# Attention vectors of the first graph layer in the tile loop, and the output projection written out by tiles with a ring for x

## The chip, the core and the metric

One core of a Trainium2 chip. The time is the device time of one execution in microseconds (us). The kernel before was run three times: 2285.08, 2288.67 and 2289.95 us, median 2288.67. One more execution was profiled.

## What is computed

A block of a graph transformer on x, 1250 nodes x 768, all in fp32. Only the mixing part and the products with the attention vectors matter here; xn is the layer norm of x.

```
# linear attention with random features (8 heads of 96, 256 features)
q, k, v = split(xn @ qkv_w.T + qkv_b);  q, k = q * scale, k * scale
phi_q, phi_k = exp(q @ rf.T - |q|^2/2), exp(k @ rf.T - |k|^2/2)
kv = phi_k^T v;  attn = (phi_q kv) / max(phi_q . sum(phi_k), 1e-6)
x1 = x + attn @ proj_w.T + proj_b (+ b2 of the graph layers)
# graph attention, first layer (4 heads of 512), second layer (1 head of 768)
al = xn @ wa,   wa[:, side, head]  = sum_c W1[:, head, c] * a_side[head, c]
al2 = h1 @ wa2, wa2[:, side]       = sum_c W2[:, c] * a2_side[c]
```

The edges' softmax and sums, the second layer, a router and 32 experts follow.

## The kernel before, in words

The 1250 nodes are 10 tiles (NT) of 125 rows (P); the 768 columns are 6 slices (KD) of 128. The program is a sequence of stages, each a block in which every engine has its own list of instructions, with waits on semaphores between them; a stage begins when all engines have ended the one before. The order in a stage is written out by hand.

The stages that matter: norm_phase; then, for each half of the heads, the tile loop of mix_half_phase (its `with ExitStack() as st1` block) and the stage `numerator`; then proj_phase; then first_layer_phase, and the rest of the network.

**Tile loop** (lines 641 to 815). For each tile TensorE (PE) multiplies xnT with the half's q, k and v weights (mix_G, L743), turns q and k (mix_TQ, L754), makes k's features (mix_PH, L762) and accumulates kv (mix_KV, L771). Between these it does two "windows" of another job, the counts of edges (mix_count_S, L791), from one-hot tiles that VectorE (DVE) writes into a ring (L667, L673). DVE's order per tile: evacuate q and k (L684), wait for ScalarE (ACT) to square them (L717), reduce to norms (L689), first window, evacuate v (L696), second window. ACT's order: squares, q's copy, counts, k's copy, exponential of the first two heads (L728), counts, exponential of the other two (L731). SyncE (SP) loads the attention vectors a (mix_a) and three 128-row slices of W1 (mix_w_slice) at the start of the stage and stores counts.

**Numerator** (L345 to L430). DVE begins with the half's 24 attention vectors: for each of 3 slices, 2 sides and 4 heads a multiply and sum over 512 columns (L413) into wa; only then does it release the two result banks R (L418, `num_used`). PE takes two heads at a time: 12 matmuls for the features of q into six banks F (L374, each two records), which ACT exponentiates (L398), then the products with kv into R (L384); DVE divides them into attn (L425 to L427). SP issues the next weights: those of half 1, and after half 1 those of the projection (L2101).

**Projection** (L433 to L566). SP loads the two biases, the whole of x (proj_x, L100 and L101), a2 and four chunks of W2 (L462), then stores the rows of x1 (L468). Per tile POOL copies attn's tile into proj_at (L476), PE turns it in six transposes into two banks (L488), ACT and DVE copy them into proj_aT (L518, L528), and PE multiplies with the weights into two banks Y (L497, 24 records). DVE adds the bias to x's row (L532), then Y (L537), and from the third tile on does four products of W2's attention columns (L555) per tile. There is one set of turn banks and one set of Y banks. PE's loop:

```
    turn(0)
    with pe.Fori(0, NT // 2 - 1) as i:
        for b in range(2):
            turn(i * 2 + (b + 1))
            project(i * 2 + b, b)
```

Of the kernel before, what the change touches and what calls it, by code (L numbers as in the profile page):

```python
# [10 lines left out]
ALU = mybir.AluOpType  # L11
# [40 lines left out]
MAX_AT = 5  # L52
NTAB = MAXT + AHEAD + 1
# [291 lines left out]
def numerator(nc, cx, tag, half, rfT, qT, kv, attn, a_loaded, slice_loaded, ws, ab, wa, load_next):  # L345
# [3 lines left out]
    KH = KD // 2  # L349
# [3 lines left out]
    wa_step = cx.sem(tag + "wa_step")  # L353
    with ExitStack() as st:
        junk = sb(nc, st, tag + "junk", [128, 2, C1])
# [46 lines left out]
        def _(dve):  # L402
            step = Chain(dve, dve_step)
            dve.wait_ge(a_loaded, 32)
            n = 0
            for k in range(KH):
                dve.wait_ge(slice_loaded[k], 16)
                for s in range(2):
                    for h in range(H1):
                        if n >= 2:  # L410
                            dve.wait_ge(wa_step, n - 1)
                        col = s * H1 + h
                        dve.tensor_tensor_reduce(out=junk[:, n % 2, :], in0=ws[k][:, h * C1:(h + 1) * C1],  # L413
                                                 in1=ab[:, s, h * C1:(h + 1) * C1], scale=1.0, scalar=0.0,
                                                 op0=ALU.mult, op1=ALU.add,
                                                 accum_out=wa[:, half * KH + k, col:col + 1]).then_inc(wa_step, 1)
                        n += 1
# [15 lines left out]
def proj_phase(nc, cx, attn, w, w_loaded, proj_b, gnn_b2, x, x1_dram, ident, W2, a_src2, a_dst2, wa2):  # L433

    (loaded, x_loaded, staged, turned, copied_a, copied_d, projected, stored, stores) = (
        cx.sem("proj_" + s) for s in ("loaded", "x_loaded", "staged", "turned", "copied_a", "copied_d", "projected",
                                      "stored", "stores"))
    biased = cx.sem("proj_biased")
    a2_loaded, wa2_step = cx.sem("proj_a2_loaded"), cx.sem("proj_wa2_step")
    KC = 4  # L440
    w2_loaded = [cx.sem(f"proj_w2_loaded{c}") for c in range(KF // KC)]
    with ExitStack() as st:
# [4 lines left out]
        xr = sb(nc, st, "proj_x", [P, NT, D])  # L447
        at = sb(nc, st, "proj_at", [P, D])
# [24 lines left out]
        def _(pool):  # L473
            with pool.Fori(0, NT) as t:
                pool.wait_ge(turned, t + 1)
                pool.tensor_copy(at[:], attn[:, bass.ds(t, 1), :]).then_inc(staged, 1)  # L476
# [1692 lines left out]
```

## Time and profile before

| | us |
|---|---|
| median of three runs | 2288.67 |
| lowest, highest | 2285.08, 2289.95 |
| the profiled execution | 2279.98 |
| its span in the trace | 2278.2 |
| busy: PE, DVE, ACT, POOL | 2102.0, 1115.7, 409.6, 184.5 |
| mean granted clock of PE, share of full | 0.951 |

Times in the trace are counted from the start of the span. A row of a timeline gives start, duration, engine, source line, operation, what it writes <- what it reads, and in brackets how long the engine had been idle before and what ended that. A row of busy times gives the stretch, its length, the busy time of PE, PE's weight loads, DVE, ACT and POOL with the number of instructions, the granted clock of PE, the busy share of the DMA engines and GB/s. An fp32 matmul leaves two records. A matmul's end is modelled, so neighbouring groups of PE can overlap by some tenths of a microsecond.

### The profile page before, as it was taken

Reading aid. Unit: us, or ns where it says so; the run is one execution under the profiler, and the core shown is the slowest. Engines: PE = TensorE matmul, PEld = TensorE weight load, DVE = VectorE, ACT = ScalarE, POOL = GpSimd, SP = SyncE. Lnnn points to the kernel's source line nnn. Section 1 sums busy time; section 2 is a strip of 40 time slices with the busy share of each in tenths; the row PEclk is TensorE's granted clock in tenths of the full one; section 3 lists DMA queues with packets and bytes.
Section 4 is the critical chain, followed back from the end, with each engine's and each line's share of the span. In section 5 each row is a group of like instructions: output and inputs, shape, how many; then the busy total and the mean of one; then the engine's idle time right before and its main releaser. Section 6 shows DMA issues by size and latency. Waiting matters only on the chain. (4 is left out here: it accounts for less than half of the span.)

```text
span 2278.2 us, 32891 instructions
## 1 busy us (share of the span) xinstructions
PE 2102.0 (92%) x9786; PEld 1455.2 (64%) x9787; DVE 1115.7 (49%) x2411; ACT 409.6 (18%) x745; POOL 184.5 (8%) x178
## 2 busy tenths in 40 slices
PE   5999899998799998899999799989966999999997
PEld 3666566666444443788888655545563777777776
DVE  6566545654454500888888300236445333333343
ACT  2211212122002311222222100000010122222221
POOL 0000000000000000000000000000001232333222
PEclk9999899999899999899999899999955899999999
DMA  7000220002634511333433354432053688898754
GB/s 240 18 15 18 82 98 18 18 17 82 200 112 134 167 53 45 121 120 94 127 98 95 124 191 148 141 101 55 11 201 119 197 245 249 247 288 253 206 130 76
DMA packets 80399, 282.26 MB, mean 124 GB/s; under 512 B 11268, under 2 KB 31292, under 8 KB 70717
## 3 DMA queue, kind: packets, MB, share of 16 engines
q1 hardware_dynamic: 59309, 216.48, 28.5%
q0 software_dynamic: 14048, 51.06, 9.7%
q10 hardware_dynamic: 6960, 13.62, 1.7%
q8 instruction: 51, 0.84, 0.2%
q14 instruction: 31, 0.25, 0.0%
HBM read 222.26 MB, written 58.87 MB: 123 GB/s over the span
## 5 line engine op out<-in xcount | busy, mean ns | idle before, releaser
L1199 PE MATMUL gat_Z<-h,gat_wt 125*125 125x256 f32 (+1 forms) x1600 | 354.8, 381 | 17.9 <-DVE gat_wt L1115 17.9
L1199 PEld LDWEIGHTS gat_Z<-h,gat_wt 125*125 125x125 f32 x1600 | 298.1, 188 | 63.5 <-DVE gat_wt L1115 18.7
L743 PE MATMUL mix_G<-mix_w,xnT 128*125 128x384 f32 x720 | 242.5, 487 | 0.0
L2017 PE MATMUL ex_PH<-ex_xT,ex_w 128*128 128x128 f32 x1872 | 223.8, 279 | 2.6 <-issue 1.1
L1347 PE MATMUL gat2p_Y<-gat2p_w,gat2p_hT 128*125 128x386 f32 (+1 forms) x640 | 209.7, 489 | 10.3 <-DMA gat2p_w<-in_L_gnn_W 10.3
L2017 PEld LDWEIGHTS ex_PH<-ex_xT,ex_w 128*128 128x128 f32 x1872 | 214.7, 193 | 4.0 <-issue 4.0
L2027 PE MATMUL ex_PY<-ex_w,ex_hT 128*128 128x384 f32 x624 | 214.8, 494 | 1.8 <-ACT ex_hT L1966 1.7
L983 PE MATMUL first_G<-gnn_w,xnT 128*125 128x512 f32 x480 | 208.4, 593 | 0.0
L743 PEld LDWEIGHTS mix_G<-mix_w,xnT 128*125 128x125 f32 x720 | 132.9, 189 | 84.5 <-issue 1.5
L1347 PEld LDWEIGHTS gat2p_Y<-gat2p_w,gat2p_hT 128*125 128x125 f32 x640 | 120.2, 188 | 98.4 <-issue 12.5
L2027 PEld LDWEIGHTS ex_PY<-ex_w,ex_hT 128*128 128x128 f32 x624 | 114.3, 190 | 77.9 <-ACT ex_hT L1966 3.4
L983 PEld LDWEIGHTS first_G<-gnn_w,xnT 128*125 128x125 f32 x480 | 89.0, 188 | 110.4 <-issue 110.4
L1461 PE MATMUL gat_Z<-h,gat_wt 125*125 125x385 f32 (+1 forms) x400 | 132.1, 493 | 9.4 <-DVE gat_wt L1419 9.4
L1461 PEld LDWEIGHTS gat_Z<-h,gat_wt 125*125 125x125 f32 x400 | 75.9, 190 | 65.6 <-DVE gat_wt L1419 10.0
L667 DVE SCALAR_TENSOR_TENSOR mix_count_A<-count_ikey,count_off,keyT 128x512 f32 x120 | 90.2, 752 | 54.0 <-issue 49.6
L673 DVE TENSOR_SCALAR mix_count_B<-count_islo,sloT 128x314 f16 x480 | 112.1, 299 | 0.0
L1937 DVE TENSOR_SCALAR ex_idS<-ex_ids 128x1 int32 x52 | 8.0, 154 | 211.4 <-DMA out_rows<-ex_y,ex_idS 211.4
L1907 DVE SCALAR_TENSOR_TENSOR ex_Q<-posm,offs,ex_iota 125x1280 bf16<-125x1280 f32 x55 | 85.4, 1552 | 42.7 <-issue 38.4
L1888 POOL DMA_INDIRECT out_rows<-ex_y,ex_idS x52 | 82.6, 1588 | 264.8 <-DVE ex_y L1939 217.1
L497 PE MATMUL proj_Y<-mix_w,proj_aT 128*125 128x384 f32 x240 | 81.9, 500 | 12.2 <-DVE proj_x L537 12.2
L791 PE MATMUL mix_count_S<-mix_count_B,mix_count_A 128*128 x480 | 86.5, 301 | 4.2 <-DVE mix_count_B L673 2.1
L1103 DVE TENSOR_TENSOR gat_u<-al,gat_rows 125x1250 f32<-125x1250 f32 x40 | 58.2, 1455 | 55.3 <-DMA gat_rows<-mT_dram 55.3
(292 smaller groups left out, 2212.9 us busy)
## 6 DMA issues: line engine op xcount, KB each, us to landing
ex_w<-in_L_ffn_W SPq DMA_DIRECT2D x64, 1152.0 KB
gat_cnt<-c_dram SPq DMA_DIRECT2D x50, 546.9 KB
gat2p_hT<-h1T_dram SPq DMA_DIRECT2D x20, 1000.0 KB, 5.0
h1T_dram<-gat_oT ACTq DMA_DIRECT2D x40, 250.0 KB, 2.0
mix_w<-in_L_mix_qkv_w SPq DMA_DIRECT2D x6, 1152.0 KB, 13.2
ct_dram<-mix_count_out SPq DMA_DIRECT2D x40, 157.0 KB, 2.2
mix_w_slice<-in_L_gnn_W SPq DMA_DIRECT2D x6, 1024.0 KB, 12.0
proj_w2s<-in_L_gnn_W SPq DMA_DIRECT2D x4, 1536.0 KB, 25.1
```

Of the source, the lines that this page charges most:

```text
L667: dve.scalar_tensor_tensor(CA[:, bass.ds(s * RB, RB), :], ikey[:].unsqueeze(1).to_broadcast([128, RB, 128]), off[:, win:win + 1], keyT[:, ...
L673: last = dve.tensor_scalar(CB[:, bass.ds(s * RB + b, 1), :], islo[:].unsqueeze(1), sloT[:, bass.ds(r * RB + b, 1)], None, ALU.is_equal)
L743: last = pe.matmul(G[c][:], xnT[:, k, t * P:(t + 1) * P], w[:, k, c, :], start=(k == 0), stop=(k == KD - 1))
L791: last = pe.matmul(S[:], CA[:, bass.ds(s * RB + b, 1), :].rearrange("p o k -> p (o k)"), CB[:, bass.ds(s * RB + b, 1), :].rearrange("p o k ...
L983: last = pe.matmul(G[g % 2][:], xnT[:, k, t * P:(t + 1) * P], w[hd % 2][:, k, :], start=(k == 0), stop=(k == KD - 1))
L1199: last = pe.matmul(Z[b][j][:], wt[b][:, s, :], h[:, s, bass.ds(hd, 1), j * HC:(j + 1) * HC + j], start=(s == 0), stop=(s == NT - 1))
L1347: last = pe.matmul(Y[b][j][:, 0:HW if j else W], hT[q % 2][:, k, :], w[:, k, cols], start=(k == 0), stop=(k == KF - 1))
L1461: last = pe.matmul(Z[b][j][:], wt[b][:, s, :], h2[:, s, 385 * j:385 * j + CW[j]], start=(s == 0), stop=(s == NT - 1))
L1888: pool.indirect_dma_start(out, bass.IndirectOffsetOnAxis(ap=idS[:, 0:1], axis=0), y[:], None, compute_op=ALU.add).then_inc(added, 16)
L1907: dve.scalar_tensor_tensor(Q[:], posm[:, :, bass.ds(e, 1)].to_broadcast([P, NT, SLOT]), offs[:, bass.ds(at, 1)], iot[:].unsqueeze(1).to_br ...
L2017: last = pe.matmul(PH[m][:], w1[:, b, k, m * 128:(m + 1) * 128], xT[:, k, :], start=(k == 0), stop=(k == KD - 1))
L2027: last = pe.matmul(PY[j][:], hT[:, k, :], w2[:, b, k, j * 384:(j + 1) * 384], start=(k == 0), stop=(k == KM - 1))
```

## The change

1. **Attention vectors.** The loop leaves `numerator` and comes into DVE's list of the tile loop, behind each tile's second window: tile t does columns t*24//10 to (t+1)*24//10 - 1, two or three. The slices of W1, a and the scratch tile now live in the tile loop's memory.
2. **Ring for x.** proj_x holds 4 tiles instead of 10 and is allocated outside the stage. `load_proj`, issued by SP in the numerator of half 1, loads the first four tiles of x behind the projection's weights. In proj_phase SP stores a tile, waits for the store and loads the tile four further on.
3. **Projection by tiles.** All loops over tiles are written out. POOL's copy is gone: PE turns attn itself. There are two sets of turn banks and two of Y banks; PE begins with turns 0 and 1, ahead of the wait for the weights, then alternates project(t) and turn(t + 2). The W2 chunks are issued one per tile instead of all four at the start.

The core of the diff:

```diff
             step = Chain(dve, dve_step)
-            dve.wait_ge(a_loaded, 32)
-            n = 0
-            for k in range(KH):
-                dve.wait_ge(slice_loaded[k], 16)
-                for s in range(2):
-                    for h in range(H1):
-                        if n >= 2:
-                            dve.wait_ge(wa_step, n - 1)
-                        col = s * H1 + h
-                        dve.tensor_tensor_reduce(out=junk[:, n % 2, :], in0=ws[k][:, h * C1:(h + 1) * C1],
-                                                 in1=ab[:, s, h * C1:(h + 1) * C1], scale=1.0, scalar=0.0,
-                                                 op0=ALU.mult, op1=ALU.add,
-                                                 accum_out=wa[:, half * KH + k, col:col + 1]).then_inc(wa_step, 1)
-                        n += 1
             dve.sem_inc(num_used, 2)
...
-        xr = sb(nc, st, "proj_x", [P, NT, D])
-        at = sb(nc, st, "proj_at", [P, D])
         aT = [sb(nc, st, f"proj_aT{b}", [128, KD, P]) for b in range(2)]
-        TP = [pb(nc, st, f"proj_T{j}", [128, 3, P]) for j in range(2)]
-        Y = [pb(nc, st, f"proj_Y{j}", [P, 384]) for j in range(2)]
+        TP = [[pb(nc, st, f"proj_T{b}{j}", [128, 3, P]) for j in range(2)] for b in range(2)]
+        Y = [[pb(nc, st, f"proj_Y{b}{j}", [P, 384]) for j in range(2)] for b in range(2)]
         block = st.enter_context(nc.Block())
 
         @block.sync
         def _(sp):
             sp.dma_start(bias[:, 0, :], proj_b.partition_broadcast(128)).then_inc(loaded, 16)
             sp.dma_start(bias[:, 1, :], gnn_b2.partition_broadcast(128)).then_inc(loaded, 16)
-            rows_dma(sp, xr, x.rearrange("(t p) d -> p t d", p=P), x_loaded)
             sp.dma_start(a2[:, 0, :], a_src2[0, :].partition_broadcast(128)).then_inc(a2_loaded, 16)
             sp.dma_start(a2[:, 1, :], a_dst2[0, :].partition_broadcast(128)).then_inc(a2_loaded, 16)
-            for c in range(KF // KC):
-                sp.dma_start(w2s[:, c * KC:(c + 1) * KC, :],
-                             W2[c * KC * 128:(c + 1) * KC * 128, :].rearrange("(k p) n -> p k n", p=128)
-                             ).then_inc(w2_loaded[c], 16)
-            with sp.Fori(0, NT) as t:
-                sp.wait_ge(stored, t * 2 + 4)
-                for lo, n in ((0, PM), (PM, P - PM)):
-                    sp.dma_start(x1_dram[bass.ds(t * P + lo, n), :],
-                                 xr[lo:lo + n, bass.ds(t, 1), :].rearrange("p o d -> p (o d)")).then_inc(stores, 16)
-            sp.wait_ge(stores, 32 * NT)
-
-        @block.gpsimd
-        def _(pool):
-            with pool.Fori(0, NT) as t:
-                pool.wait_ge(turned, t + 1)
-                pool.tensor_copy(at[:], attn[:, bass.ds(t, 1), :]).then_inc(staged, 1)
+            for t in range(NT):
+                b = t % XR
+                if t < KF // KC:
+                    sp.dma_start(w2s[:, t * KC:(t + 1) * KC, :],
+                                 W2[t * KC * 128:(t + 1) * KC * 128, :].rearrange("(k p) n -> p k n", p=128)
+                                 ).then_inc(w2_loaded[t], 16)
+                sp.wait_ge(summed, 2 * t + 2)
+                rows_dma(sp, x1_dram[t * P:(t + 1) * P, :], xr[:, b, :], stores[b])
+                if t + XR < NT:
+                    sp.wait_ge(stores[b], 32 * (t // XR + 1))
+                    rows_dma(sp, xr[:, b, :], x[(t + XR) * P:(t + XR + 1) * P, :], x_loaded[b])
+            for b in range(XR):
+                sp.wait_ge(stores[b], 32 * len(range(b, NT, XR)))
 
         @block.tensor
         def _(pe):
-            pe.sem_inc(turned, 1)
-            pe.sem_inc(projected, 4)
-
             def turn(t):
-                pe.wait_ge(staged, t + 1)
+                b = t % 2
+                if t >= 2:
+                    pe.wait_ge(copied_a, t - 1)
+                    pe.wait_ge(copied_d, t - 1)
+                for k in range(KD):
+                    last = pe.transpose(TP[b][k // 3][:, k % 3, :], attn[:, t, k * 128:(k + 1) * 128], ident[0:P, 0:P])
+                last.then_inc(turned, 1)
+
+            def project(t):
+                b = t % 2
                 pe.wait_ge(copied_a, t + 1)
                 pe.wait_ge(copied_d, t + 1)
-                for k in range(KD):
-                    last = pe.transpose(TP[k // 3][:, k % 3, :], at[:, k * 128:(k + 1) * 128], ident[0:P, 0:P])
-                last.then_inc(turned, 1)
-
-            def project(t, b):
-                pe.wait_ge(copied_a, t + 2)
-                pe.wait_ge(copied_d, t + 2)
                 for j in range(2):
-                    pe.wait_ge(stored, 2 * t + (j + 1))
+                    if t >= 2:
+                        pe.wait_ge(summed, 2 * (t - 2) + (j + 1))
                     for k in range(KD):
-                        last = pe.matmul(Y[j][:], aT[b][:, k, :], w[:, k, j * 384:(j + 1) * 384],
+                        last = pe.matmul(Y[b][j][:], aT[b][:, k, :], w[:, k, j * 384:(j + 1) * 384],
                                          start=(k == 0), stop=(k == KD - 1))
                     last.then_inc(projected, 1)
 
+            turn(0)
+            turn(1)
             pe.wait_ge(w_loaded, 16)
-            turn(0)
-            with pe.Fori(0, NT // 2 - 1) as i:
-                for b in range(2):
-                    turn(i * 2 + (b + 1))
-                    project(i * 2 + b, b)
-            turn(NT - 1)
-            project(NT - 2, 0)
-            project(NT - 1, 1)
+            for t in range(NT):
+                project(t)
+                if t + 2 < NT:
+                    turn(t + 2)
 
         @block.scalar
         def _(act):
-            act.sem_inc(copied_a, 1)
-            with act.Fori(0, NT // 2) as i:
-                for b in range(2):
-                    act.wait_ge(turned, i * 2 + (b + 2))
-                    act.wait_ge(projected, i * 4 + (2 * b + 2))
-                    act.activation(aT[b][:, 0:3, :], TP[0][:], ACT.Copy).then_inc(copied_a, 1)
+            for t in range(NT):
+                act.wait_ge(turned, t + 1)
+                if t >= 2:
+                    act.wait_ge(projected, 2 * (t - 1))
+                act.activation(aT[t % 2][:, 0:3, :], TP[t % 2][0][:], ACT.Copy).then_inc(copied_a, 1)
...
             def add(t):
-                row = xr[:, bass.ds(t, 1), :]
-                dve.tensor_tensor(row, row, bias[0:P, 0:1, :], ALU.add).then_inc(biased, 1)
+                row = xr[:, t % XR, :]
+                dve.wait_ge(x_loaded[t % XR], 32 * (t // XR + 1))
+                dve.tensor_tensor(row, row, bias[0:P, 0, :], ALU.add).then_inc(biased, 1)
                 dve.wait_ge(biased, t + 2)
                 for j in range(2):
-                    dve.wait_ge(projected, 2 * t + (j + 5))
-                    col = xr[:, bass.ds(t, 1), j * 384:(j + 1) * 384]
-                    dve.tensor_tensor(col, Y[j][:].unsqueeze(1), col, ALU.add).then_inc(stored, 1)
-
-            turn(0, 0)
-            turn(1, 1)
-            dve.wait_ge(loaded, 32)
-            dve.tensor_tensor(bias[:, 0, :], bias[:, 0, :], bias[:, 1, :], ALU.add).then_inc(biased, 1)
-            dve.wait_ge(x_loaded, 32)
-            dve.wait_ge(biased, 1)
+                    dve.wait_ge(projected, 2 * t + (j + 1))
+                    col = xr[:, t % XR, j * 384:(j + 1) * 384]
+                    dve.tensor_tensor(col, Y[t % 2][j][:], col, ALU.add).then_inc(summed, 1)
...
+            turn(0)
+            turn(1)
+            dve.wait_ge(loaded, 32)
+            dve.tensor_tensor(bias[:, 0, :], bias[:, 0, :], bias[:, 1, :], ALU.add).then_inc(biased, 1)
+            dve.wait_ge(biased, 1)
             for t in range(NT):
                 add(t)
                 if t + 2 < NT:
-                    turn(t + 2, t % 2)
+                    turn(t + 2)
                 if t >= 2:
                     for k in range(2 * (t - 2), 2 * (t - 1)):
                         attention_columns(k)
-
 
...
+                    def attention_column(n):
+                        k, col = n // (2 * H1), n % (2 * H1)
+                        side, hd = col // H1, col % H1
+                        if n == 0:
+                            dve.wait_ge(a_loaded, 32)
+                        if col == 0:
+                            dve.wait_ge(slice_loaded[k], 16)
+                        if n >= 2:
+                            dve.wait_ge(wa_step, n - 1)
+                        dve.tensor_tensor_reduce(out=junk[:, n % 2, :], in0=ws[k][:, hd * C1:(hd + 1) * C1],
+                                                 in1=ab[:, side, hd * C1:(hd + 1) * C1], scale=1.0, scalar=0.0,
+                                                 op0=ALU.mult, op1=ALU.add,
+                                                 accum_out=wa[:, half * KH + k, col:col + 1]).then_inc(wa_step, 1)
+
+                    columns = 2 * H1 * KH
                     pair = ((q_done, q_turned, q_evac, qsq, q_ready), (k_done, k_turned, k_evac, ksq, k_ready))
                     for t in range(NT):
...
                                           brow[0:P, 2, :].rearrange("p (h d) -> p h d", d=MD), ALU.add
                                           ).then_inc(v_evac, 1)
                         window(PER * t + 1)
+                        for n in range(t * columns // NT, (t + 1) * columns // NT):
+                            attention_column(n)
                 dve.wait_ge(kv_step, NT)
...
                 rfT = sb(nc, st2, "mix_rfT", [MD + 1, RF])
+                xr = sb(nc, st2, "proj_x", [P, XR, D])
+                xr_loaded = [cx.sem(f"proj_x_loaded{b}") for b in range(XR)]
                 counting = (sb(nc, st2, "count_ikey", [128, 128]), sb(nc, st2, "count_islo", [128, SLO], F16),
                             sb(nc, st2, "count_off", [128, NW]), sb(nc, st2, "count_zero", [128, 128], BF16))
                 w_proj = w_qkv[:, :, 0:2, :].rearrange("p k c n -> p k (c n)")
                 def load_proj(eng):
                     eng.dma_start(w_proj, ins["L0_mix_proj_w"].rearrange("(k p) n -> p k n", p=128)
                                   ).then_inc(proj_loaded, 16)
+                    for t in range(XR):
+                        rows_dma(eng, xr[:, t, :], x[t * P:(t + 1) * P, :], xr_loaded[t])
 
```

## Rows read from the trace of the kernel before

**Rows 1.** The page's busy times: busy us, share, number of instructions.

```profile
PE 2102.0 (92%) x9786; PEld 1455.2 (64%) x9787; DVE 1115.7 (49%) x2411; ACT 409.6 (18%) x745; POOL 184.5 (8%) x178
```

**Rows 2.** Busy times by stretch, 540 to 600 us; engines, granted clock, DMA share, GB/s.

```profile
540.00:600.00 60.00, 43.93 (x193) 29.64 (x193) 13.58 (x28) 8.15 (x16) 4.12 (x5) 0.86 0.67 201
```

**Rows 3.** PE's timeline, half 0's numerator and entry of half 1: start us, us, what.

```profile
256.56 10.36 PE L374 MATMUL mix_F<-mix_qT,mix_rfT 97*128 x24 [1.91 <-ACTq L391]
269.95 10.61 PE L384 MATMUL mix_R<-mix_kv,mix_phiq 128*125 x80 [3.03 <-DVEq L418]
280.40 8.59 PE L374 MATMUL mix_F<-mix_qT,mix_rfT 97*128 x24
288.83 8.87 PE L384 MATMUL mix_R<-mix_kv,mix_phiq 128*125 x80
300.33 1.57 PE L777 MATMUL mix_KV<-mix_vs,mix_zero 125*128 125x388 f32 x4 [2.63 <-POOL mix_vs L646]
```

**Rows 4.** Busy times by stretch, three stretches of 2 us after a pause.

```profile
272.00:274.00 2.00, 2.00 (x12) 2.00 (x11) 0.81 (x3) 0.00 (x0) 0.00 (x0) 0.50 0.00 0
...
302.00:304.00 2.00, 2.00 (x7) 1.12 (x6) 0.00 (x0) 0.00 (x0) 0.00 (x0) 1.00 1.03 422
...
562.00:564.00 2.00, 1.79 (x7) 1.64 (x8) 0.24 (x1) 0.16 (x1) 0.26 (x2) 0.50 0.83 180
```

**Rows 5.** Timeline, half 1's numerator.

```profile
529.72 10.60 PE L384 MATMUL mix_R<-mix_kv,mix_phiq 128*125 x80 [3.01 <-DVEq L418]
```

**Rows 6.** Groups of instructions of 255 to 272 us: busy us, mean ns.

```profile
L413 DVE CUSTOM_DVE_ANT_0 mix_junk<-mix_w_slice,mix_a 128x512 f32<-128x512 f32 x24 | 14.8, 685 | 0.5 <-PEq L604 0.5
...
L413 DVE DVE_READ_ACCUMULATOR2_ANT gnn_wa<- 128x1 f32 x24 | 1.9, 80 | 0.0
```

**Rows 7.** Timeline, PE from the output projection to the next stage's first matmul.

```profile
560.33 0.83 PE L488 MATMUL proj_T<-ident,proj_at 125*128 125x125 f32 x6 [2.86 <-POOL proj_at L476]
...
585.10 10.01 PE L497 MATMUL proj_Y<-mix_w,proj_aT 128*125 128x384 f32 x24 [12.16 <-DVE proj_x L537]
...
595.59 7.91 PE L497 MATMUL proj_Y<-mix_w,proj_aT 128*125 128x384 f32 x24
...
645.90 15.65 PE L497 MATMUL proj_Y<-mix_w,proj_aT 128*125 128x384 f32 x48
...
667.22 14.66 PE L989 MATMUL mask_T<-xnT,gnn_wa 128*8 128x416 f32 x36 [5.67 <-PEq L94]
```

**Rows 8.** Timeline, DVE's first work on x in the output projection.

```profile
583.50 0.96 DVE L532 TENSOR_TENSOR proj_x<-proj_x,proj_bias 125x768 f32<-125x768 f32 x1 [17.11 <-DMA proj_x<-in_x]
```

**Rows 9.** Busy times by stretch, the output projection once it runs evenly.

```profile
604.00:645.00 41.00, 41.00 (x146) 24.74 (x145) 31.54 (x60) 2.41 (x5) 4.14 (x5) 1.00 0.15 47
```

**Rows 10.** Timeline of one tile of half 0's tile loop.

```profile
144.97 0.55 DVE L684 SCALAR_TENSOR_TENSOR mix_qs<-mix_G,mix_brow 125x384 f32<-125x384 f32 x1
...
146.37 0.56 DVE L684 SCALAR_TENSOR_TENSOR mix_qs<-mix_G,mix_brow 125x384 f32<-125x384 f32 x1 [0.86 <-PE mix_G L743]
...
150.67 0.60 ACT L731 ACTIVATE mix_phik<-mix_PH 125x512 f32<-125x512 f32 x1 [0.50 <-PE mix_PH L762]
...
151.71 0.55 DVE L689 TENSOR_REDUCE mix_nrm<-mix_sq 125x4 f32<-125x384 f32 x1 [4.78 <-ACT mix_sq L717]
...
156.10 0.59 PE L754 MATMUL mix_TQ<-ident,mix_qs 125*97 125x125 f32 x4
```

**Rows 11.** Line L689's idle time and releaser: us, times.

```profile
  ACT mix_sq L717: 86.0, 18
```

**Rows 12.** DVE's timeline, end of half 1's tile loop.

```profile
514.48 1.03 DVE L702 COPY mix_kv<-mix_KV 128x388 f32<-128x388 f32 x2 [7.21 <-PE mix_KV L771]
```

**Rows 13.** DMA issues: number, KB each, median us from issue to landing.

```profile
mix_w_slice<-in_L_gnn_W SPq DMA_DIRECT2D x6, 1024.0 KB, 12.0
proj_w2s<-in_L_gnn_W SPq DMA_DIRECT2D x4, 1536.0 KB, 25.1
...
mix_w<-in_L_mix_proj_w SPq DMA_DIRECT2D x1, 2304.0 KB, 8.2
```

More of the change, by code:

```diff
@@ L52 @@
 MAX_AT = 5
+XR = 4
 NTAB = MAXT + AHEAD + 1
@@ L342, in _, with numerator @@
                 last.then_inc(transposed, 1)
-def numerator(nc, cx, tag, half, rfT, qT, kv, attn, a_loaded, slice_loaded, ws, ab, wa, load_next):
-    KH = KD // 2
+def numerator(nc, cx, tag, half, rfT, qT, kv, attn, load_next):
     HH, A, HT = MH // 2, MD + 1, NT // 2
@@ L430, in _, with proj_phase @@
             step.end(HH // 2)
[L433 to L438, printed above, removed]
+def proj_phase(nc, cx, attn, w, w_loaded, proj_b, gnn_b2, x, xr, x_loaded, x1_dram, ident, W2, a_src2, a_dst2, wa2):
+    (loaded, turned, copied_a, copied_d, projected, summed, biased) = (
+        cx.sem("proj_" + s) for s in ("loaded", "turned", "copied_a", "copied_d", "projected", "summed", "biased"))
     a2_loaded, wa2_step = cx.sem("proj_a2_loaded"), cx.sem("proj_wa2_step")
+    stores = [cx.sem(f"proj_stores{b}") for b in range(XR)]
     KC = 4
@@ L520, in _, with turn @@
         @block.vector
         def _(dve):
-            dve.sem_inc(copied_d, 1)
-            dve.sem_inc(stored, 2)
-            def turn(t, b):
-                dve.wait_ge(turned, t + 2)
-                dve.wait_ge(projected, 2 * t + 2)
-                dve.tensor_copy(aT[b][:, 3:6, :], TP[1][:]).then_inc(copied_d, 1)
+            def turn(t):
+                dve.wait_ge(turned, t + 1)
+                if t >= 2:
+                    dve.wait_ge(projected, 2 * (t - 1))
+                dve.tensor_copy(aT[t % 2][:, 3:6, :], TP[t % 2][1][:]).then_inc(copied_d, 1)
@@ L550, in attention_columns @@
                     dve.wait_ge(a2_loaded, 32)
-                for s in range(2):
-                    n = 2 * k + s
+                for side in range(2):
+                    n = 2 * k + side
                     if n >= 2:
                         dve.wait_ge(wa2_step, n - 1)
-                    dve.tensor_tensor_reduce(out=junk[:, s, :], in0=w2s[:, k, :], in1=a2[:, s, :], scale=1.0,
+                    dve.tensor_tensor_reduce(out=junk[:, side, :], in0=w2s[:, k, :], in1=a2[:, side, :], scale=1.0,
                                              scalar=0.0, op0=ALU.mult, op1=ALU.add,
-                                             accum_out=wa2[:, k, s:s + 1]).then_inc(wa2_step, 1)
+                                             accum_out=wa2[:, k, side:side + 1]).then_inc(wa2_step, 1)
+            turn(0)
[3 more added lines that the diff above has]
+            dve.wait_ge(biased, 1)
             for t in range(NT):
@@ L601, in mix_half_phase @@
         kv = sb(nc, st, tag + "kv", [128, HH, 2, A])
-        ws = [sb(nc, st, tag + f"w1_slice{k}", [128, F1]) for k in range(KD // 2)]
-        ab = sb(nc, st, tag + "a", [128, 2, F1])
         with ExitStack() as st1:
+            ws = [sb(nc, st1, tag + f"w1_slice{k}", [128, F1]) for k in range(KH)]
+            ab = sb(nc, st1, tag + "a", [128, 2, F1])
+            junk = sb(nc, st1, tag + "junk", [128, 2, C1])
             qs = sb(nc, st1, tag + "qs", [P, 2, HH, A])
@@ L816, in _ @@
                         keys_values(t, not more)
-        numerator(nc, cx, tag, half, rfT, qT, kv, attn, a_loaded, slice_loaded, ws, ab, wa, load_next)
+        numerator(nc, cx, tag, half, rfT, qT, kv, attn, load_next)
 def first_layer_phase(nc, cx, W1, xnT, wa, ident, al, alT_dram, ct_dram, c_dram, mask_dram, mT_dram, h):
```

9 lines of the change are left out of this document (4 added, 5 removed).

## The prediction

> **What bounds the kernel now.** I read the page's busy times first: TensorE (PE) is busy for 92% of the span [rows 1], so time can be won only where PE stands still or runs at a low clock. The busy times by stretch come next. They show the worst stretch of the part that the diff touches: between 540 and 600 us PE is busy for 43.93 us of 60, at a mean granted clock of 0.86, while the DMA engines are 67% busy [rows 2]. Last I read the order of work there.
>
> In the numerator of half 0, PE ends its feature matmuls (mix_F) at 256.56 + 10.36 = 266.92. Its next group (mix_R) starts at 269.95, after 3.03 us of waiting for VectorE's (DVE's) sequencer at L418, which is the line behind the 24 attention vectors [rows 3]. The same group takes 10.61 us the first time and 8.87 the second [rows 3]; in between lies a stretch at a granted clock of 0.50, which is 1.2 of 2.4 GHz [rows 4]. Half 1 repeats this: 3.01 us of wait, then 10.60 us [rows 5]. The vectors are 24 instructions of DVE with a mean of 685 ns, and as many short reads of the accumulator of 80 ns, which overlap their neighbours: 14.8 us for the 24 [rows 6].
>
> In the output projection, PE starts its first transposes at 560.33 after waiting for POOL's copy. It stands still for 12.16 us before 585.10, until DVE has added the first tile, and the 24 matmuls that follow take 10.01 us where undisturbed ones take 7.91 [rows 7]. DVE itself had waited 17.11 us for the load of x [rows 8]. From 604 us on there is no wait: PE is busy for 41.00 of 41.00 us, DVE for 31.54 [rows 9].
>
> **Part 1, the attention vectors leave the numerator.** DVE then reaches L418 at once. The ACT engine's last exponentials feed the second head, not the first group, so nothing else holds mix_R, as in the second pass, where it starts 0.16 us before the modelled end of mix_F [rows 3]. Gone are the gaps, 3.03 + 3.01 us. With no gap there is no cause for the low clock behind it: I price mix_R at the 8.87 us of its second pass, which saves 1.74 + 1.73 us more. Sum: 9.5 us. The first mix_F pass keeps its 10.36 us against 8.59 [rows 3], for the gap ahead of it stays. If the low clock stays too, 6.0 us is left; more than 9.5 has no source, since PE has no other gap there. I take 9.5, because the second pass is the same code without the wait.
>
> **Part 2, the same vectors go into the tile loop.** Each tile gets 2 or 3 of the 24, that is 14.8 / 24 = 0.62 us each, 1.2 to 1.9 us a tile, issued by DVE after its second window. What DVE does next is evacuate q and k (144.97 and 146.37) and then stand idle for 4.78 us until ACT has squared them [rows 10]; ACT cannot square before its exponential at 150.67 is over [rows 10]. So k may be evacuated some 4 us later than 146.9 without anyone being late. That idle time is 86.0 us in 18 tiles, 4.8 us each [rows 11]: it covers 1.9 us in every tile. PE's own turn of q comes at 156.10, 3.6 us after DVE's norm is ready at about 152.5 [rows 10]. In the tenth tile there is no next q; there the vectors lie in the 7.21 us in which DVE waits for the last keys-values group [rows 12]. The added waits (for the slices and a) guard loads that are issued when the half starts and land in 12.0 us [rows 13]; the first vector comes at the end of the first tile, and a tile takes about (514.48 - 300.33) / 10 = 21.4 us [rows 3, 12]. Cost: 0. If the cover were gone, DVE's 48 x 0.62 = 29.5 us would be paid; a gain is excluded, as work is only added. I take 0, since the cover is over twice the cost in each tile.
>
> **Part 3, the projection by tiles.** POOL's copy and its wait go; turns read attn itself. The PE entry of the stage is then that of SP and POOL, which I put at 559.2 (POOL's copy of 0.83 us ends just ahead of 560.33). Two turns of 0.83 us [rows 7] end at 560.9, and DVE's and ACT's first copies are done by then, as they start when the first turn ends. PE then runs without a gap: the period of a tile is (645.90 - 595.59) / 6 = 8.385 us, and the last two take 15.65 together [rows 7]. With 8 periods and that pair the matmuls end at 560.9 + 67.1 + 15.65 = 643.6 instead of 661.55: 17.9 us earlier. By its pieces this is 2.6 (start), 12.2 (x), 2.1 (10.01 to 7.91) and 0.9 (the first group was slow as well). The tail to the next stage's first matmul at 667.22 [rows 7], with the last W2 columns on DVE, is as before.
>
> What holds this up: the x ring's first four tiles are loaded behind the projection's weights in the numerator of half 1. These weights land in 8.2 us [rows 13], and the numerator takes some 45 us, from 514.48 to 560.33 [rows 7, 12], so 8 more issues on SP's queue and 1.5 MB are hidden. The bias still arrives late, but the second pair of Y banks lets PE go on to tile 2 before it needs a sum. DVE is busy for 77% of a steady stretch [rows 9], so unrolled it keeps up. SP now sends a W2 chunk, a store, a wait for that store and a refill per tile; a refill has three periods, 25 us.
>
> Open is the clock at the start. The pause ahead of the stage shrinks from 2.86 us to 1.7. After 2.86 us (and 1.05 more at POOL) the clock read 0.50 at 562, while after a pause of 2.63 us at 300.33 it read 1.00 [rows 3, 4]. I charge nothing, since the new pause is shorter than the harmless one; the bound is one low spell, 1.7 us as in mix_R. The Trainium skill ("TensorE: Matmul & The Clock Gate", Part 1) says that idle time throttles the clock and that the point where it turns differs from run to run. By that the spell would be paid in some runs and the sum would be 1.7 us smaller in them; the rows show both outcomes and don't decide.
>
> **Sum.** 9.5 + 0 + 17.9 = 27.4 us. Everything later is untouched and moves as a block. The profiled execution took 2279.98 us, so it would take 2252.6. The median of the runs, 2288.67, is 8.7 us above it; I subtract from the median: 2261.3 us.
>
> **Rivals.**
> 1. The gaps go, but low clock spells stay or a start is cold: 6.0 + 16.2 = 22.2 us, 2266.5. For it: a low spell also follows some short pauses [rows 4]. Against: the second mix_R pass.
> 2. SP's queue becomes the bound of the projection. A W2 chunk now took 25.1 us to land [rows 13]. If that were still so with one chunk a tile, and the next store and refill stood behind it, four chunks would end at 561 + 100.4 = 661.4, the last columns on DVE some 7 us later, and the stage would end no earlier than now: only 8 to 9.5 us are left, 2280. It decides from about (643.6 - 561) / 4 = 20 us a chunk. Against: the 25.1 us are those of four chunks issued together behind the whole of x, by the shapes 6.3 + 3.8 MB; one chunk is 1.6 MB, and the stretch is 83 us long. The Trainium skill ("DMA: Bandwidth & Descriptors", Queues, rings and completion order) states that each DMA engine takes the descriptors of a ring in order, which is what puts a store behind its chunk; the rows show no store in such a place.
> 3. The other side: DVE paces the tile loop. If the idle time before the norm were no cover (because q's chain, not ACT, sets PE's turn), each vector would cost its full 0.69 + 0.08 us [rows 6], 48 of them 36.8 us; less 27.4, this is 9.4 us slower, 2298.1. It decides only once the cover of 4.8 us falls below 1.9.
> 4. mix_R waits for something else than the vectors, or the edit merely moves the wait: 17.9 us are left, 2270.8. Against: the releaser named is DVE's sequencer, twice [rows 3, 5].
>
> **Chances.** Forecast 0.73, rival 1 0.14, rival 4 0.03, rival 2 0.05; these are all faster by over 0.2% (4.6 us, about what a measurement of this kernel can tell from no change). A mixture that ends within 0.2% has 0.02, rival 3 0.03. The range runs from 2253, the profiled execution less 27.4, since runs differ by such an amount, to 2270, which takes in rival 1 with the spread of the runs and nearly rival 4.
>
> **What would show it.** Right: mix_R starts where mix_F ends, in both halves, and takes 8.9 us; DVE's idle time before L689's norm shrinks from 4.8 to about 3 us and mix_G's rhythm stays at 20 to 21 us a tile; the projection's matmuls run without a gap over some 83 us. Wrong: PE waits before its turn of q, or DVE in the projection waits for W2 or x, or a low clock between the groups of mix_R.

## The result, and the profile after

| | before | after | ratio |
|---|---|---|---|
| first comparison, median of 4 runs each | 2287.22 us | 2257.1 us (2249.7 to 2263.36) | 0.9889, 95% interval 0.9849 to 0.9929 |
| second comparison (after_again, below) | 2285.67 us | 2259.94 us | 0.9892, 0.9875 to 0.991 |
| the profiled execution; its span | 2279.98; 2278.2 | 2253.74; 2252.0 | |

The kernel is 30.1 us faster by the first medians, 25.7 by the second and 26.2 between the two profiled executions; 27.4 were forecast. One of the ten executions of vectors_only below took 7752.69 us, for a reason that is not known; its ratio and interval leave it out.

PE's timeline of half 0's numerator and the entry of half 1, in the changed kernel (before: [rows 3]):

```profile
257.04 12.05 PE L372 MATMUL mix_F<-mix_qT,mix_rfT 97*128 x24 [1.91 <-ACTq L389]
268.93 8.87 PE L382 MATMUL mix_R<-mix_kv,mix_phiq 128*125 x80
277.64 8.59 PE L372 MATMUL mix_F<-mix_qT,mix_rfT 97*128 x24
286.07 8.87 PE L382 MATMUL mix_R<-mix_kv,mix_phiq 128*125 x80
297.57 2.53 PE L766 MATMUL mix_KV<-mix_vs,mix_zero 125*128 125x388 f32 x4 [2.63 <-POOL mix_vs L618]
...
525.75 8.87 PE L382 MATMUL mix_R<-mix_kv,mix_phiq 128*125 x80
```

mix_R now starts at the end of mix_F and takes 8.87 us in both halves: the wait and the low clock behind it are gone, as forecast. But the first mix_F pass took 12.05 us instead of 10.36, and the zeroing at the entry of half 1 takes 2.53 instead of 1.57. Both lie at the low clock. Busy times by stretch (the column behind POOL's is the granted clock; before, 302 to 304 us read 1.00 [rows 4]):

```profile
260.00:262.00 2.00, 2.00 (x4) 0.96 (x3) 0.00 (x0) 0.93 (x2) 0.00 (x0) 0.50 0.97 323
298.00:300.00 2.00, 2.00 (x5) 1.05 (x4) 0.00 (x0) 0.00 (x0) 0.00 (x0) 0.51 0.90 377
```

The tile of the tile loop that answers to [rows 10], on the timeline, and L676's idle time (the line of the norm, L689 before [rows 11]):

```profile
145.21 0.68 DVE L659 CUSTOM_DVE_ANT_0 mix_junk<-mix_w_slice,mix_a 128x512 f32<-128x512 f32 x1
...
147.04 1.02 DVE L671 SCALAR_TENSOR_TENSOR mix_qs<-mix_G,mix_brow 125x384 f32<-125x384 f32 x2
...
151.96 0.55 DVE L676 TENSOR_REDUCE mix_nrm<-mix_sq 125x4 f32<-125x384 f32 x1 [3.90 <-ACT mix_sq L706]
...
156.35 0.59 PE L743 MATMUL mix_TQ<-ident,mix_qs 125*97 125x125 f32 x4
```

```profile
  ACT mix_sq L706: 70.0, 18
```

Three vectors, 1.8 us of work from 145.21 on, stand between the window and q's evacuation, and PE's turn comes 0.25 us later than before, in a loop that runs 0.25 us later as a whole. The idle time before this norm fell by only 0.88 us (4.78 to 3.90), because DVE also had 0.86 us of idle time before k's evacuation [rows 10], which is gone. In all the cover shrank from 86.0 to 70.0 us and is not used up.

PE's timeline of the projection, and the stretch that answers to [rows 2]:

```profile
553.41 1.47 PE L463 MATMUL proj_T<-ident,attn 125*128 125x125 f32 x12 [1.65 <-PEq L353]
554.98 7.98 PE L474 MATMUL proj_Y<-mix_w,proj_aT 128*125 128x384 f32 x24
...
571.82 7.91 PE L474 MATMUL proj_Y<-mix_w,proj_aT 128*125 128x384 f32 x24
...
622.13 15.65 PE L474 MATMUL proj_Y<-mix_w,proj_aT 128*125 128x384 f32 x48
643.46 14.10 PE L978 MATMUL mask_T<-xnT,gnn_wa 128*8 128x416 f32 x36 [5.69 <-PEq L95]
```

```profile
540.00:600.00 60.00, 58.26 (x261) 38.89 (x260) 28.14 (x56) 6.08 (x13) 0.00 (x0) 1.00 0.52 176
```

No wait is left between the first turn and the last matmul. To see where time went, I cut each trace at the same seven matmuls of PE: A is the first mix_F of half 0, B the zeroing of half 1, C the mix_KV that ends half 1's first tile, D the first mix_F of half 1, E the first turn of the projection, F the first matmul of the next stage (mask_T). All in us, worked out from the starts in the timelines, one profiled execution of each kernel:

| kernel | A to B | B to C | C to D | D to E | E to F | F to the end |
|---|---|---|---|---|---|---|
| before | 43.77 | 33.34 | 182.68 | 43.98 | 106.89 | 1610.98 |
| after | 40.53 | 35.09 | 182.90 | 37.85 | 90.05 | 1608.54 |
| after_again | 38.84 | 35.07 | 185.57 | 38.51 | 91.40 | 1611.21 |
| vectors_only | 38.84 | 35.04 | 185.59 | 39.80 | 107.85 | 1613.44 |
| projection_only | 43.77 | 33.35 | 182.95 | 42.77 | 90.05 | 1612.68 |
| x_in_stage | 38.84 | 35.08 | 185.52 | 38.63 | 91.40 | 1612.58 |
| x_whole_in_stage | 39.58 | 34.81 | 185.57 | 38.33 | 103.29 | 1609.38 |
| w2_columns_earlier | 38.85 | 35.07 | 185.58 | 38.56 | 90.78 | 1612.88 |

Of the 26.2 us between the profiled spans, 16.8 come from the projection, 6.1 from half 1's numerator up to the first turn (1.2 of them because POOL's copy no longer stands before that turn) and 3.2 from half 0's numerator. The way to A gave back 0.5, B to C 1.75 and C to D 0.2. The 2.4 us behind F belong to work that was not touched, which differs by up to 4.9 us between the traces of the table.

### The profile page after: what moved, and what is told of

Read it like the earlier page. It is cut to its first block and busy times, and to the rows that moved or that the text cites. A ratio compares the mean times of both kernels' runs of the same rounds, so it can differ in the third digit from the quotient of the medians.

```text
span 2252.0 us, 32723 instructions
## 1 busy us (share of the span) xinstructions
PE 2095.8 (93%) x9786; PEld 1450.2 (64%) x9787; DVE 1113.4 (49%) x2411; ACT 409.1 (18%) x745; POOL 180.1 (8%) x168
## 5 line engine op out<-in xcount | busy, mean ns | idle before, releaser
L1188 PE MATMUL gat_Z<-h,gat_wt 125*125 125x256 f32 (+1 forms) x1600 | 354.4, 381 | 17.9 <-DVE gat_wt L1104 17.9
L1963 ACT ACTIVATE ex_y<-ex_PY,ex_gate 128x384 f32<-128x384 f32 x52 | 30.2, 581 | 281.5 <-DMA out_rows<-ex_y,ex_idS 243.8
## 6 DMA issues: line engine op xcount, KB each, us to landing
mix_w_slice<-in_L_gnn_W SPq DMA_DIRECT2D x6, 1024.0 KB, 11.1
```

The lines of the kernel that those rows point to most:

```text
L1188: last = pe.matmul(Z[b][j][:], wt[b][:, s, :], h[:, s, bass.ds(hd, 1), j * HC:(j + 1) * HC + j], start=(s == 0), stop=(s == NT - 1))
```

## The experiments

Diffs are against the changed kernel, where nothing else is said.

**after_again: the changed kernel once more.**

> The changed kernel once more, unchanged. Theory (waits removed, plus the low clock behind them): 26 to 30 us faster than before; the numerator's first mix_F pass takes 10.4 or 12.1 us and the start of half 1 may be at the low clock or not, since both were seen in the two traces so far. Rival (the clock spells are a fixed result of the new order of work): the first mix_F pass of half 0 takes 12.05 us and mix_KV's zeroing 2.53 us again, as in the first trace of after.

2259.94 us (2259.35 to 2263.76), ratio 0.9892: 25.7 us faster by the medians, just under the 26 to 30 expected. The first mix_F pass took 10.36 us this time, so its 12.05 was no fixed result; the zeroing of half 1 took 2.86. The last mix_KV of half 1 took 3.73 us where the first trace has 2.03, and half 1's first mix_F pass, behind it, 11.02 us instead of 10.36. A spell in that tile was not new: in before it lay some microseconds earlier, on mix_PH (507.30, 2.07 us instead of the 1.13 of after). The spells differ from run to run in the first case; the one at B came again.

**vectors_only: part 1 and 2 of the change alone.** The projection and its loads are those of before.

> Only the attention vectors move into the tile loop, the projection is that of before. Theory: mix_R starts where mix_F ends, 3.0 us sooner in each half, and takes 8.87 us instead of 10.6: 9.5 us faster less low clock spells elsewhere, so 6 to 9.5 us. Rival (the vectors are paid for in the tile loop): 0.62 us for each of the 48 comes back, 29.5 us, and the kernel is 20 us slower than before. Rival 2 (the clock spell only moves to another place): 6 us.

2279.0 against 2285.67 us, ratio 0.9968 (0.9955 to 0.998): 6.7 us faster by the medians. PE's timeline shows both halves of the mechanism, and what came in their place:

```profile
257.84 10.36 PE L372 MATMUL mix_F<-mix_qT,mix_rfT 97*128 x24 [1.91 <-ACTq L389]
268.04 8.87 PE L382 MATMUL mix_R<-mix_kv,mix_phiq 128*125 x80
...
296.68 2.74 PE L780 MATMUL mix_KV<-mix_vs,mix_zero 125*128 125x388 f32 x4 [2.63 <-POOL mix_vs L632]
...
511.65 3.73 PE L774 MATMUL mix_KV<-mix_vs,mix_phik 125*128 125x97 f32 x16 [0.69 <-ACT mix_phik L734]
```

A to B is 4.9 us shorter; B to C gives 1.7 back and C to D 2.9. Of the 2.9, 2.6 lie in the last tile and the pause behind it, where the granted clock is low:

```profile
508.00:512.00 4.00, 3.31 (x11) 1.88 (x10) 0.00 (x0) 1.03 (x2) 0.00 (x0) 0.57 0.11 40
512.00:516.00 4.00, 3.37 (x16) 3.13 (x15) 0.59 (x2) 0.00 (x0) 0.00 (x0) 0.50 0.00 0
```

The first rival (all is paid in the loop) falls; the second (the clock spell moves) is in good part right.

**projection_only: part 3 alone.** The 24 vectors per half stay in the numerator.

> Only the projection is rewritten; the vectors stay in the numerator. Theory: the stage from mix_R's end to the next stage's first matmul is 17.9 us shorter and the kernel 17 to 19 us faster; mix_R still waits 3.0 us in each half. Rival (the two parts depend on each other, since the numerator of half 1 must hide the x loads while DVE is late): less than 17 us.

2265.18 us, ratio 0.9912 (0.9894 to 0.993): 20.5 us faster. E to F is 16.84 us shorter and D to E 1.21, together 18.05; mix_R waits 3.03 and 3.01 us as before. The two parts add up within the intervals: 6.7 + 20.5 = 27.2 us by the medians against 25.7 for both.

**Which piece of the projection removed the wait for x?** Three kernels take back the early load, the second set of Y banks, and both.

```diff
# x_in_stage: load_proj loads no x; SP, behind the two biases of the stage:
+            for t in range(XR):
+                rows_dma(sp, xr[:, t, :], x[t * P:(t + 1) * P, :], x_loaded[t])
# one_y_set: one pair of banks, so each project(t) waits for the sum of t - 1
-                    if t >= 2:
-                        pe.wait_ge(summed, 2 * (t - 2) + (j + 1))
+                    if t >= 1:
+                        pe.wait_ge(summed, 2 * (t - 1) + (j + 1))
# x_in_stage_one_y: both
```

> The changed kernel, but the ring's first four tiles of x are loaded at the start of the projection, behind the biases, as the whole of x was before. Theory (the early load removed the 12.2 us): the projection from its first turn to the next stage's first matmul is longer than 90.05 us by the part of that wait that four tiles bring, 3 us or more. Rival (the second set of Y banks removed it): PE needs the first sum only at its third tile, 17 us into the stage, when four tiles (1.5 MB) have long landed, so the stage stays at 90 to 91 us.

> The changed kernel with one set of Y banks in place of two; x is loaded early. Theory (early load): the first sums end 8.1 and 10.0 us after the first turn, bound by the bias, so PE waits at most 1 us at its second tile and the stage is 90 to 91.5 us. Rival (banks): PE stands still once per tile for DVE's sum, 0.5 us or more in each of 10 tiles, 95 us or more.

> Both taken back: one set of Y banks, and x loaded in the stage. If either alone suffices, this one brings PE's wait back: x's first tile lands some 10 us after the stage begins and the first sum follows at 12 us or later, so PE waits 2 to 5 us before its second tile, perhaps with a low clock behind it: 93 to 97 us. If the wait of before came from the order of the loads alone (all of x in one transfer), it stays at 91.

E to F is 91.40, 91.39 and 91.40 us (whole kernels, one run each: 2260.48, 2263.16 and 2264.17 us). Neither piece is needed, and not even one of the two. For x_in_stage the theory (early load) was wrong; its rival had about the right time (91.40 for 90 to 91) for the wrong reason, since the stage stays as short with one set of banks too. x_in_stage_one_y did what was expected for the case that all of x in one transfer had been the cause. The timeline of x_in_stage shows why: DVE waits 0.45 us for the first tile of x, behind the bias that it has to wait for anyway.

```profile
560.82 0.96 DVE L530 TENSOR_TENSOR proj_bias<-proj_bias 128x768 f32<-128x768 f32 x1 [3.23 <-DMA proj_bias<-in_L_gnn_b]
562.23 0.96 DVE L507 TENSOR_TENSOR proj_x<-proj_x,proj_bias 125x768 f32<-125x768 f32 x1 [0.45 <-DMA proj_x<-in_x]
```

The 1.35 us above after's 90.05 are the low clock at the start of the stage: the twelve transposes take 2.28 us and the first 24 matmuls 8.82, against 1.47 and 7.98. after_again, where nothing was changed, has the same 91.40. So the start of the stage is at the low clock in some executions of one kernel and not in others. The prediction cited the Trainium skill ("TensorE: Matmul & The Clock Gate", Part 1) for the clock's turning point differing from run to run; the two traces of this kernel agree with it.

**x_whole_in_stage: the load of before in the new projection.** All ten tiles with one semaphore, at the start of the stage; nothing is loaded in the numerator, and nothing is refilled.

```diff
+            rows_dma(sp, xr, x.rearrange("(t p) d -> p t d", p=P), x_loaded)
-                dve.wait_ge(x_loaded[t % XR], 32 * (t // XR + 1))
+                dve.wait_ge(x_loaded, 32)
```

> The changed kernel's projection, with x loaded as before: all ten tiles in one transfer with one semaphore, at the start of the stage. Theory (what cost 12.2 us was that the first sum waited for all of x): x lands 15 to 24 us into the stage as it did before, the first sum comes then, PE waits for it before its third tile, 18 us into the stage, and a low clock follows: stage of 92 to 100 us against 91.4. Rival (the rest of the rewriting, by tiles and with two sets of banks, removed the wait whatever the load): 90 to 91.5.

E to F is 103.29 us (whole kernel 2271.22 us, one run), above the 92 to 100 expected and 11.9 more than the 91.4 of x_in_stage, which differs from it in the load of x alone; that is about the 12.2 of [rows 7]. In the timeline DVE waits 18.85 us for x; its copy of the third turn is queued behind that add, and PE waits 8.91 us for the copy and then takes 10.70 us instead of 7.91, at the low clock:

```profile
583.08 0.96 DVE L507 TENSOR_TENSOR proj_x<-proj_x,proj_bias 125x768 f32<-125x768 f32 x1 [18.85 <-DMA proj_x<-in_x]
```

```profile
585.65 10.70 PE L476 MATMUL proj_Y<-mix_w,proj_aT 128*125 128x384 f32 x24 [8.91 <-DVE proj_aT L502]
```

So the step that pays is that x no longer comes as ten tiles at once with one semaphore. Two things go together in that step: the first sum waits for one tile only, and fewer bytes (four tiles, 1.5 MB, in place of 3.84) are under way ahead of it. No run separates them; ten transfers with ten semaphores, or four tiles with one, would. Two sets of banks did not help: the copy of the turn stands behind the late sum on DVE.

**w2_at_start: the four W2 chunks issued together, as before.**

> The changed kernel with all four W2 chunks issued at the start, as before. Rival 2 of the prediction (the queue holds stores and refills behind W2): SP is still busy issuing at 20 us, the first store goes out then, the refills of x come late and DVE waits for x or PE for a sum: the stage grows by 2 us or more. Theory: a refill has three tile periods, 25 us, of slack, so the stage stays at 90 us, and the chunks' order of issue is worth nothing.

E to F is 91.40 us (2264.91 us, one run). The refill of x's fifth tile went out 26.7 us after the first turn instead of 14.8, and still nobody waited. SP's own rows show why it is late: the store ahead of it takes 3.10 us to issue behind the four chunks, and SP goes on 12.0 us after it issued the store's second part.

```profile
569.96 3.10 SPq L101 DMA_DIRECT2D x_dram<-proj_x  x1
573.11 0.96 SPq L102 DMA_DIRECT2D x_dram<-proj_x  x1
585.14 0.32 SPq L101 DMA_DIRECT2D proj_x<-in_x  x1
```

In the changed kernel, with one chunk ahead, the same wait for the store is 4.3 us (563.95 to 568.25). The chunks themselves took 12.2 to 20.4 us to land, against 9.1 when issued one per tile. That agrees with the rule of the Trainium skill ("DMA: Bandwidth & Descriptors", Queues, rings and completion order) that the prediction named, that a DMA engine takes a ring's descriptors in order, but the delay is smaller than a refill's slack. Rival 2 of the prediction falls in its strong form too. That the chunks were not what made x late before is shown by x_whole_in_stage, where x was late with a single chunk behind it.

**vectors_x5: each vector computed five times.**

> The changed kernel with each of the 48 attention vectors computed five times in the tile loop (the four extra results go to a scratch column). Theory (cover): a tile's DVE path has 4.2 us until ACT squares and 1.8 us more until PE needs the first window's tiles; tiles with two vectors add 6.2 us and stay almost free, tiles with three add 9.3 and cost 3 us each: some 13 us in each half's tile loop, 25 us in all. Rival 3 of the prediction (no cover, every vector is paid): 4 x 29.5 us, 118 us. A third reading, that DVE is nowhere near the bound, gives 0.

2300.29 us (one run, before 2284.17). C to D is 202.36 us against 185.57 in after_again, and the stretch from the first zeroing to A is 237.97 against 219.05: 35.7 us for some 118 us of added work (192 more vectors of 0.62 us). The cover is real and has a limit: some 82 us of that work are hidden, where I expected 93. The waits between 60 and 252 us show the bound moving to DVE. In the first row ACT waits for the evacuation of q and k; in the second PE waits for the norm. Neither wait is there in this stretch in before or after:

```profile
ACT mix_sq L708 <- DVE mix_qs L673: 25.2, 9, 5.3
...
PE mix_TQ L745 <- DVE mix_qs L679: 3.7, 3, 1.6
```

Computed once, the vectors cause no such wait; five times, they cost 35.7 us. Rival 3 of the prediction (every vector paid) falls.

**w2_columns_earlier: no W2 column behind the last tile.**

```diff
-                if t >= 2:
-                    for k in range(2 * (t - 2), 2 * (t - 1)):
+                if 1 <= t <= KF // 2:
+                    for k in range(2 * (t - 1), 2 * t):
```

> The changed kernel with the W2 attention columns begun one tile earlier, so that none is left behind the last tile. Theory (the stage's tail of 5.7 us holds 3.5 us of these columns): the stage is 86.5 to 88 us instead of 90.05 or 91.4, the kernel 2 to 3.5 us faster than the changed one. Rival (the tail is set by the last store's landing, which SP waits for): the stage is shorter by under 1 us.

2259.92 against 2284.17 us, ratio 0.9893 (0.9878 to 0.9909), the same as the changed kernel; E to F 90.78, 0.6 us less than 91.40, where at least 2 were expected. The rival was right: SP issues the last store of x1 at 641.62 and waits for its landing, and the next stage begins at 645.68. DVE's tail lay beside that.

**zero_later, on top of w2_columns_earlier.** PE begins the tile loop with the q and k products; the zeroing of mix_KV, which waits for POOL's memsets, follows.

```diff
-                pe.wait_ge(consts, 2)
-                for j in range(2):
-                    pe.matmul(KV[j]...)
...
                     gemm(1, 0, k_done, k_evac)
+                    pe.wait_ge(consts, 2)
+                    for j in range(2):
+                        pe.matmul(KV[j]...)
```

> As w2_columns_earlier, and the zeroing matmuls of mix_KV come behind the q and k products of the first tile, so PE need not wait for POOL's memsets (2.97 and 2.63 us before mix_KV). Theory: PE starts each half's loop about 1 us sooner, 2 us in all. Rival (the wait is the block's entry and not the memset, or the weights set it): nothing.

2250.98 us, ratio 0.9855 (0.984 to 0.987), 8.9 us less than w2_columns_earlier on the same chip. Only part of it was expected (1 us in each half): PE idles 1.93 us instead of 2.63 at the entry of half 1, as its timeline shows.

```profile
255.98 8.66 PE L372 MATMUL mix_F<-mix_qT,mix_rfT 97*128 x24 [1.91 <-ACTq L389]
...
292.43 7.98 PE L732 MATMUL mix_G<-mix_w,xnT 128*125 128x384 f32 x24 [1.93 <-PEq L353]
300.24 1.47 PE L788 MATMUL mix_KV<-mix_vs,mix_zero 125*128 125x388 f32 x4
```

Most of the rest is the clock. A to C takes 69.25 us here and 73.9 in w2_columns_earlier, C to D 183.6 against 185.6, D to F 127.3 against 129.3. In A to C the first mix_F pass gives 1.7 us, the zeroing 1.3 (2.76 to 1.47) and the pause 0.7; the last mix_KV of half 1 takes 2.03 us instead of 3.73, and the projection starts at full speed. The first mix_F pass is at full speed behind the same pause of 1.91 us that in before went with 10.36. This trace does not say why.

**keep_warm, on top of zero_later.** PE ends each tile loop with 12 short matmuls and each numerator with 3, into banks that nothing reads any more.

```diff
+                    pe.wait_ge(s_evac, PER * NT)
+                    for _ in range(12):
+                        pe.matmul(S[:], czero[:], islo[:], start=True, stop=True, skip_group_check=True)
...
+            pe.wait_ge(exped, 6 * HH + 6)
+            for j in range(3):
+                pe.matmul(F[j][:, 0:CHW[0]], rfT[:, 0:128], qT[:, 0, 0:CHW[0]], start=True, stop=True)
```

> As zero_later, and PE fills its time at the end of each tile loop with 12 short matmuls and at the end of each numerator with 3, whose results nothing reads. Theory (the low clock after each stage border follows from PE's idle time there): the first mix_F pass falls from 10.4 or more towards 8.6 us and the start of half 1 and of the projection loses its spell, 2 to 6 us in all. Rival (the border's remaining idle time is enough for the clock to fall): the spells stay or only move, and the time is that of zero_later within 2 us.

2249.49 us, ratio 0.9845 (0.9831 to 0.9858), the fastest kernel of this study and 1.5 us below zero_later, inside their intervals. Both first mix_F passes run at full speed:

```profile
258.07 8.67 PE L372 MATMUL mix_F<-mix_qT,mix_rfT 97*128 x24 [0.81 <-ACTq L392]
...
511.07 8.67 PE L372 MATMUL mix_F<-mix_qT,mix_rfT 97*128 x24 [0.81 <-ACTq L392]
```

In half 1, zero_later still had 10.36 there; D to E is 36.94 us against 37.85. The pause there is 0.81 us instead of 1.90. The starts of half 1 and of the projection were at full speed in zero_later already, so nothing was left to win there. The filler is paid too: the two profiled spans are 2249.5 us here and 2249.2 in zero_later. The time is what the rival expected, within 2 us of zero_later, though the one spell named by the theory did go. Whether keep_warm beats zero_later in the mean stays open.

## Why the prediction was right, point by point

- **Part 1, the gaps.** Right to the tenth: 3.03 and 3.01 us are gone, and mix_R takes 8.87 us in every trace without the vectors in the numerator.
- **Part 1, the low clock: mis-sized.** The step "with no gap there is no cause for the low clock behind it" held for mix_R, but the 3.5 us were not kept. In all traces with the vectors moved and the zeroing first, B to C is 34.8 to 35.1 us; in both with the vectors in the numerator it is 33.34 and 33.35. C to D was 2.6 to 3.0 us longer in all of them but the first trace of after and vectors_x5, whose C to D holds the added work, and the first mix_F pass differed too. From A to E, part 1 brought 4.5 us in vectors_only (303.8 to 299.3), and, against projection_only's 302.8, 6.5 us in after, 4.8 in after_again and 3.9 in one_y_set, x_in_stage_one_y and w2_at_start, whose first mix_F pass took 11.5 us, where 9.5 were forecast. By the medians of vectors_only it is 6.7. The term belongs between 4 and 7, mostly under the low bound of 6.0 that the prediction kept for this case. In this rival 1 was nearer than the forecast.
- **Part 2, nothing paid in the loop.** Right. No wait of PE for DVE's norm appears. From C to the second last mix_KV of half 1 it is 165.9 us in after, 166.0 in projection_only, where no vectors are in the loop, and 165.6 in before. Five times the work shows the limit. The sign "4.8 to about 3 us" of idle time was mis-sized: it is 3.9 (70.0 us in 18 tiles), since the 0.86 us before k's evacuation were cover too.
- **Part 3, 17.9 us.** Right in size: 16.84 + 1.21 = 18.05 in after. With the low clock at the start, which I charged nothing, it is 16.7 in after_again and the five other traces with both parts and an E to F of 91.4; the bound of one spell (1.7 us) contained it at 1.35. The pieces were wrongly reasoned: what "holds this up" was neither the early load of the ring nor the second set of Y banks, but that x is no longer loaded as ten tiles with one semaphore.
- **The sum.** 27.4 forecast, 25.7 and 30.1 by the medians. That it came so near is in part luck. The change touches only what lies before F, and F comes 23.8 us earlier in after and 20.8 in after_again (667.22 to 643.46 and to 646.39): 3.6 and 6.6 us under the forecast, which are mostly part 1's surplus and the low clock at the projection's start. The medians show more than these traces because before's profiled execution (2279.98 us) was faster than all 13 of its runs in the second comparison (median 2285.67); in which stage the slower executions of before lose these 5.7 us, no trace shows. By the traces rival 1's 22.2 us are as near as the forecast or nearer; by the medians the forecast is. Rivals 3 and 4 did not occur, and rival 2 was tested and fell. Rival 3's price has a slip that changes nothing: 48 x 0.77 is 37.0 us, not 36.8.

## What to carry to other kernels

Before paying for a ring or a second set of buffers, ask which bytes the first consumer needs, load them ahead of the rest and give them a semaphore of their own: here going from ten tiles with one semaphore to single tiles was worth 11.9 of the projection's 18 us. The load ahead of the stage and the second set of Y banks brought nothing that could be measured. Work that is moved into another engine's idle time is free as long as it lies between a wait that ends late anyway and its consumer; multiply it by five to see the limit. Don't book the low clock behind a removed pause as gain: it may come back in a later stretch, and only a trace of the whole shows it.

## What the runs showed of the hardware that was not expected

- The same pause of 1.90 or 1.91 us before the first mix_F pass went with passes of 8.66, 10.36 and 12.05 us. The granted clock stayed at 1.00 (2.4 GHz) in the first case (zero_later). In before it read 0.52 and 0.63 in the two stretches from 258 to 262 us, and in after, with 12.05 us, 0.50, 0.50 and 0.52 in the three from 258 to 264 (1.2 GHz). So the length of the pause does not decide it. What PE did before differed between these kernels by little that I can name; it stays open.
- In the last tile of half 1, where PE has short matmuls with pauses of 0.3 to 0.7 us, the clock fell to the low level in after_again and vectors_only (mix_KV 3.73 us instead of 2.03) without any long pause.
- The spells go together over some 50 us. In the nine traces in which that last mix_KV takes 3.73 us, the mix_F pass behind it takes 10.8 to 11.1 us, and the projection starts at the low clock (twelve transposes in 2.3 to 2.6 us; in vectors_only the first six in 1.48 instead of 0.83). In after, projection_only, zero_later and keep_warm it takes 2.03 us, the pass 10.36 or 8.67, and the transposes 1.47. So the spells of one execution must not be priced as if each fell by itself. What sets the pattern stays open.
- The whole of x, 3.84 MB in one pair of transfers, landed some 23.6 us after its issue in before, with four W2 chunks behind it, and 25.4 us after it in x_whole_in_stage, with a single chunk (559.92 to 583.50 and 557.64 to 583.08); a chunk of W2 (1.5 MB) lands in 9.1 us in the changed kernel. Why x is so slow was not tried.
